# A cross-attention kernel: where GpSimd's sums of output weights, its head sums and its query powers stand

## The chip, the cores and the metric

The kernel runs on one core of a Trainium2 chip. The metric is device time in microseconds of one execution, median of several; the profile is of one further execution, which has a time of its own. The engines are TensorE (PE, with its weight loads PEld), VectorE (DVE), ScalarE (ACT), GpSimd (POOL) and SyncE (SP), which here issues almost every DMA in the order of its program.

## The reference, cut to what matters

```python
def _L0_xattn_ref(latents, context, Wq, Wk, Wv, Wo, q_norm_w, k_norm_w):   # 8 batches, 100 latents, 361 context rows
    kv = jnp.concatenate([context, latents], axis=1)                       # 461 keys
    q = (latents @ Wq)...            # 32 heads of 128
    k = (kv @ Wk)... ; v = (kv @ Wv)...                                    # 8 key heads, 4 query heads on each
    q = rms_norm(q, q_norm_w); k = rms_norm(k, k_norm_w)
    probs = jax.nn.softmax(einsum(qg, k) * scale)
    out = einsum(probs, v).reshape(bsz, q_len, HEADS * HEAD_DIM)
    return out @ Wo
x = x + jnp.tanh(g_xattn[0]) * _L0_xattn_ref(_layernorm(x), ctx_4096, ...)
x = x + jnp.tanh(g_ffn[0]) * _L0_ffn_ref(_layernorm(x), ...)               # router, top 2 of 8 experts of rank 16
```

## The kernel before, in words

Everything is float32. An operand is split into a high and a low part of TensorE's fp32r type (hi by ACT, lo = raw - hi by DVE), and a product is three matmuls (lines 973 to 975: hi*hi, hi*lo, lo*hi). The work has three stages.

**Keys and values** (until about 640 us). Seven Winograd products for each tile of rows. The keys and values go to DRAM (`kT_d`, `v_d`).

**Attention by units** (about 640 to 1470 us). A unit u is one key head and one batch (`UNITS` = 64 of them), and has four query heads. A query block n (`query_part(n, c)`, c = 0 to 7, n = 0 to 63) makes one query head for four batches, so two blocks share one head's weights, which SP loads (`load_wq`), and ACT and DVE split (`wq_split`). Nine blocks (`AHEAD`) are made before unit 0; then slot u of each engine's program holds the scores of unit u, the transposes and values of unit u-1, and query block u+9. In a slot:
- PE: `scores(u, i)` for the four heads into two banks, `turn_probs(u-1, t)` (transposes of the probabilities), `values(u-1, t)`, `query_part` and `squares` (a head's sums of squares).
- DVE (`slot`, for u below 55): `maxima(u, i)` (line 1923, and `nm` = -max * rq, line 1929), `inverse(u, i)` (`rr`, line 1938), `p_split(u-1, t)` (`pT_lo`, line 1917), `copy_queries`, and at the end of the slot `mean_squares` (`ms`, line 1887), `q_split(u+1)` (`q_lo`, line 1897) and, when u is odd and below 52, `next_wq` (`wq_lo`, line 1805). `scores(u+1, 0)` waits for `q_lo` of u+1.
- ACT: `exps(u, i)` waits for `nm`; `p_split`, `q_split`, `keep_attn(u-1)`.
- POOL: `scale(u, i)` (line 901) multiplies a head's probabilities by `rr` as soon as it is there. `turn_probs(u, 0)` in slot u+1 waits for all four. `unit_rms` (line 896) is the power -0.5 for four units at a time (`rq`), which `nm` needs. Before every fourth unit it stands ahead of that slot's scales. It waits for `ms`.

**The output product** by Winograd (from slot 56 on, alone after 1450 us). It wants sums of quarters of Wo and of attention outputs. These are made early, on POOL, between the scales:
- `weight_sum(i)`, i = 0 to 63 (line 912): step n = i // 4 of `WT_STEPS` = 16 takes one MB. SP loads it (`load_t(n)`, line 713) to one of two buffers `tb[:, n % 2]`, POOL makes four sums in place, and SP stores it (`store_t(n)`, line 717, to `wt_d`). `load_t(n)` for n >= 2 waits until the store of n-2 has landed; `store_t(n)` waits until the sums are made. `WT_AT` says after which slot's scales a sum stands: four ahead of slot 0 and behind `unit_rms(0)`, then one a slot and in every sixth slot or so two, until slot 50.
- `early_sum(n)`, n = 0 to 15 (line 918): a difference of two units' outputs (S3), loaded and stored by SP, one a slot behind the scales of slot 35 + n (`S3_AT` = 34 is the slot of the first load).

An engine works its program off in order, and a wait holds all behind it. Before unit 0, SP's program is: the last stores of keys, the loads of keys and values for units 0 and 1, `load_heads(n)` for n = 0 to 8 (which gives `load_wq(4)` at n = 5 and `load_wq(5)` at n = 7), with `load_t(0)` and `load_t(1)` at n = 7 (`AHEAD - 2`). `next_wq(7)` splits head 5's weights on ACT and DVE. On ACT it stands ahead of `q_split(0)`, and on DVE ahead of `mean_squares(6)`.

Of the kernel before, what the change touches and what calls it, by code (L numbers as in the profile page):

```python
# [15 lines left out]
B = 8  # L16
# [17 lines left out]
TB = B // 2  # L34
# [94 lines left out]
UNITS = G * B  # L129
AHEAD = 9  # L130
# [17 lines left out]
WT_OF = {P6: 0, P4: 1, P7: 2, P5: 3}  # L148
WT_OPS = ((2, 3, 2, True), (0, 2, 0, False), (3, 3, 0, True), (1, 1, 0, True))
WT_STEPS = GQ * R  # L150
WT_AT = {}
for _n in range(4 * WT_STEPS):
    WT_AT.setdefault(max(-1, (_n - 4) * 6 // 7), []).append(_n)
WT_DONE = {n: next(u for u in WT_AT if 4 * n + 3 in WT_AT[u]) for n in range(WT_STEPS)}

S3_AT = 34
S3_STEPS = GQ * TB

UPPER = (P5, P4)
TAIL0 = FIRST_OF[P2]  # L160
# [11 lines left out]
def build(nc, x, ctxT, Wq, Wkv, Wo, AR, BmT, vecs, rows, out):  # L172
    with ExitStack() as ctx:
        def sem(name):
            return ctx.enter_context(nc.semaphore(name))
# [203 lines left out]
        nm_done = sem("nm_done")  # L379
# [89 lines left out]
        def stored(u):  # L469

            return 16 * (u // 2 + 1)
# [29 lines left out]
        def _(sp):  # L501
# [112 lines left out]
            def load_kT(u):  # L614
                g, b = u // B, u % B
                if u >= 2:
                    sp.wait_ge(s_done, 4 * (u - 2) + 4)
                r0 = b // TB * ROWS_M + b % TB * NC
                l0 = b // TB * ROWS_M + CTX_M + b % TB * NQ
                src = kT_d[:, g]  # L620
                sp.dma_start(kT[:, u % 2, :, 0:NC].bitcast(F32), src[:, :, r0:r0 + NC]).then_inc(kT_in[u % 2], 16)
                sp.dma_start(kT[:, u % 2, :, NC:NK].bitcast(F32), src[:, :, l0:l0 + NQ]).then_inc(kT_in[u % 2], 16)

            def load_vv(u):
                g, b = u // B, u % B
                if u >= 2:
                    sp.wait_ge(pv_done, u - 1)
                r0 = b // TB * ROWS_M + b % TB * NC
                l0 = b // TB * ROWS_M + CTX_M + b % TB * NQ
                dst = vv[:, u % 2].bitcast(F32)  # L630
                sp.dma_start(dst[0:ROWS[0], 0], v_d[r0:r0 + ROWS[0], g]).then_inc(vv_in[u % 2], 16)
                sp.dma_start(dst[0:ROWS[1], 1:3], v_d[r0 + OFF[1]:r0 + NC, g].rearrange("(t r) l d -> r t l d", t=2)
                             ).then_inc(vv_in[u % 2], 16)
                sp.dma_start(dst[0:NQ, 3], v_d[l0:l0 + NQ, g]).then_inc(vv_in[u % 2], 16)

            def store_attn(u):
                sp.wait_ge(ao_done, u + 1)
                sp.dma_start(at_d[u // B, u % B], ao[:, u % 2]).then_inc(ao_stored[u % 2], 16)
# [13 lines left out]
            def load_heads_of(m):  # L652
# [6 lines left out]
                if m < 2:  # L659
                    for i in range(4):  # L660
                        sp.wait_ge(s3_stored[i], 16 * S3_STEPS // 4)
                elif o in (P5, P6) and c >= 2 or m - 2 > LAST_OF[P6]:
# [27 lines left out]
            def load_chunk(m):  # L690
                load_weights(m)
                load_heads_of(m)

            def load_s3(n):
                if n >= 4:
                    sp.wait_ge(s3_stored[n % 4], 16 * (n // 4))
                for th in range(2):
                    u = n // TB * B + th * TB + n % TB
                    sp.wait_ge(ao_stored[u % 2], stored(u))
                    sp.dma_start(s3b[n % 4][th], at_d[u // B, u % B]).then_inc(s3_in[n % 4], 16)  # L700

            def store_s3(n):
                sp.wait_ge(s3_sum, n + 1)
                sp.dma_start(s3_d[n // TB, :, n % TB], s3b[n % 4][0]).then_inc(s3_stored[n % 4], 16)
# [5 lines left out]
            def load_t(n):  # L710
                if n >= 2:
                    sp.wait_ge(t_stored[n % 2], 16 * (n // 2))
                sp.dma_start(tb[:, n % 2], Wo.rearrange("n (k c) p r d -> c r p (n k) d", k=2)[n // R, n % R]).then_inc(t_in[n % 2], 16)

            def store_t(n):
                sp.wait_ge(t_sum, 4 * n + 4)
                sp.dma_start(wt_d.rearrange("t c p r d -> c r p t d")[n // R, n % R], tb[:, n % 2]).then_inc(t_stored[n % 2], 16)
# [10 lines left out]
            def load_heads(n):  # L728

                h = n // 2 + 2  # L730
                if n % 2 == 1 and 4 <= h < H:
                    load_wq(h)

            for n in range(AHEAD):
                load_heads(n)
                if n == AHEAD - 2:
                    load_t(0)
                    load_t(1)
            for u in range(UNITS):
                load_heads(u + AHEAD)  # L740
                if 1 <= u < UNITS - 1:
                    load_kT(u + 1)

                for n in range(WT_STEPS):
                    if u == WT_DONE[n] + 1:
                        store_t(n)
                    if u == WT_DONE[n] + 2 and n + 2 < WT_STEPS:
                        load_t(n + 2)
                if 0 <= u - S3_AT - 2 < S3_STEPS:
                    store_s3(u - S3_AT - 2)  # L750
                if 0 <= u - S3_AT < S3_STEPS:
                    load_s3(u - S3_AT)
                if u in (OUT0 - 2, OUT0 - 1):
                    load_chunk(u - OUT0 + 2)
                if OUT0 + 1 <= u:
                    load_chunk(u - OUT0 + 1)
                if u == UNITS - 1:
                    load_heads_of(G + 2)
                    load_heads_of(G + 3)
                if u >= 1:  # L760
                    store_attn(u - 1)
                    if u + 1 < UNITS:
                        load_vv(u + 1)
# [50 lines left out]
        def _(pool):  # L814
# [76 lines left out]
            def unit_rms(u):  # L891

                g, b = u // B, u % B
                pool.wait_ge(ms_done, 2 * g + b // TB + 1)
                c = slice(R * b, R * (b + TB))
                pool.tensor_tensor(rq[0:NQ, g, c], ms[0:NQ, c], mhalf[0:NQ, 0:R * TB], ALU.pow).then_inc(rq_done, 1)

            def scale(u, i):
                a = 4 * u + i
                pool.wait_ge(rr_done, a + 1)  # L900
                pool.tensor_scalar(pr[0:NQ, u % 2, i], pr[0:NQ, u % 2, i], rr[0:NQ, i:i + 1], None,  # L901
                                   ALU.mult).then_inc(p_done, 1)

            def weight_sum(i):

                n = i // 4
                to, a, b, minus = WT_OPS[i % 4]
                if i % 4 == 0:
                    pool.wait_ge(t_in[n % 2], 16 * (n // 2 + 1))
                elif i % 4 < 3:  # L910
                    pool.wait_ge(t_sum, i)
                pool.tensor_tensor(tb[:, n % 2, to], tb[:, n % 2, a], tb[:, n % 2, b],
                                   ALU.subtract if minus else ALU.add).then_inc(t_sum, 1)

            def early_sum(n):

                pool.wait_ge(s3_in[n % 4], 32 * (n // 4 + 1))
                pool.tensor_tensor(s3b[n % 4][0], s3b[n % 4][0], s3b[n % 4][1], ALU.subtract).then_inc(s3_sum, 1)

            def chunk_sums(m):  # L920

                o, c = CHUNKS[m]
                pool.wait_ge(at_in[m % 4], a_loaded(m))
                if o == P6:
                    pool.wait_ge(at_sum, summed(m - 1))
                to, x, y = {P5: (a21[c % 2], a21[c % 2], a22[c % 2]), P6: (a11[c % 2], a21[c % 2], a11[c % 2]),
                            P3: (at_raw[m % 2], at_raw[m % 2], at_more[:, m % 2])}[o]
                for b in range(TB):
                    pool.tensor_tensor(to[:, b], x[:, b], y[:, b], ALU.add if o == P5 else ALU.subtract).then_inc(at_sum, 1)

            unit_rms(0)
            for i in WT_AT[-1]:
                weight_sum(i)
            for u in range(UNITS):
                if u % TB == TB - 1 and u + 1 < UNITS:
                    unit_rms(u + 1)
                for i in range(R):
                    scale(u, i)
                for i in WT_AT.get(u, ()):
                    weight_sum(i)  # L940
                if 0 <= u - S3_AT - 1 < S3_STEPS:
                    early_sum(u - S3_AT - 1)
                if u == UNITS - 2:
                    chunk_sums(FIRST_OF[P5])
            for m in range(FIRST_OF[P6], LAST_OF[P6] + 1):
# [1249 lines left out]
```

## Time and profile before

| | us |
|---|---|
| median of 3 runs | 1715.18 |
| lowest and highest | 1713.99, 1717.83 |
| the profiled execution's own time | 1715.65 |
| its span in the profile | 1713.8 |
| busy in the span: PE, DVE, POOL, ACT | 1665.8, 1239.6, 873.9, 865.1 |
| scores of unit 0 begin | 684.61 |
| scores of unit 51 begin | 1281.26 |

Times in the rows are microseconds from the start of the span. The profiled execution's time is 0.47 us above the median and 1.85 us above its own span. In the views by time a row gives start, duration, engine (a q behind it marks the queue that issues), line, operation, what is written and read, shapes and count, and in brackets the idle time before it with what ended it. Several instructions of a kind without a pause between them share a row. The view by stretches gives the stretch, its length, then busy time and count for PE, PEld, DVE, ACT and POOL, then PE's granted clock (1.00 is full), the DMA engines' busy share and GB/s. In it PE's busy time counts matmuls in their modelled length.

### The profile page before, as it was taken

What the parts mean: (1) busy time and instruction counts of PE and PEld (TensorE: products, weight loads), DVE (VectorE), ACT (ScalarE), POOL (GpSimd) and SP (SyncE); (2) the same over time, 40 slices, a digit from 0 to 9 for tenths busy, and PEclk for the clock granted to TensorE, in tenths of its full rate; (3) what the DMA queues carried; (4) which work ended last, traced back from release to release, by engine and by line L of the source; (5) the groups of instructions that cost most, each with busy time, mean ns of one, the idle gap of its engine ahead of it and who ended that gap; (6) DMA issues with size and microseconds to landing.
All of it is one profiled execution on the core that took longest, in us unless ns stands there. A gap on an engine that the chain in (4) does not pass through costs nothing.

```text
span 1713.8 us, 26112 instructions
## 1 busy us (share of the span) xinstructions
PE 1665.8 (97%) x9120; PEld 1475.3 (86%) x9120; DVE 1239.6 (72%) x2078; ACT 865.1 (50%) x1647; POOL 873.9 (51%) x668
## 2 busy tenths in 40 slices
PE   7999999999999999999999999999999999999996
PEld 6788888678888869899999999999999889999994
DVE  7788776677777742777777777777776876557767
ACT  5445554454444432555666565665555666443321
POOL 1454444134443320766767667788786445543320
PEclk9999999999999999999999999999999999999998
DMA  5667778636666564456555554666756557676632
GB/s 196 161 181 233 235 210 241 183 108 186 162 184 154 140 239 150 138 159 191 188 156 187 182 179 160 213 217 216 232 181 215 170 205 267 212 275 229 241 116 68
DMA packets 238502, 323.86 MB, mean 189 GB/s; under 512 B 53300, under 2 KB 193396, under 8 KB 233380
## 3 DMA queue, kind: packets, MB, share of 16 engines
q1 hardware_dynamic: 237796, 315.65, 59.8%
q10 hardware_dynamic: 576, 6.55, 0.9%
q8 instruction: 73, 1.20, 0.3%
q14 instruction: 57, 0.47, 0.1%
HBM read 212.18 MB, written 109.97 MB: 188 GB/s over the span
## 4 chain that ended last, share of the span: by engine, by line
PE 70%; DVE 18%; issue 4%; ACT 4%; DMA 2%; POOL 0%; DVEq 0%; SPq 0%; ACTq 0%; POOLq 0%
PE bank L973 21%; PE bank L975 20%; PE bank L974 20%; DVE mx L1923 4%; PE bank L1111 3%; DVE wq_lo L1805 3%; DVE q_lo L1897 3%; PE bank L1078 2%; DVE pT_lo L1917 2%; DMA kT_d<-kst 1%; PE bank L1007 1%; ACT pr L1539 1%; DVE q_raw L1875 1%; DVE nm L1929 1%; DVE wo_lo L1943 1%
## 5 line engine op out<-in xcount | busy, mean ns | idle before, releaser
L901 POOL TENSOR_SCALAR pr<-pr,rr 100x461 f32<-100x461 f32 x256 | 370.2, 1454 | 231.6 <-DVE rr L1938 231.6
L973 PE MATMUL bank<-w_hi,a_hi 128*128 128x512 f32 (+1 forms) x856 | 340.8, 398 | 11.7 <-DVE a_lo L1713 8.6
L975 PE MATMUL bank<-w_hi,a_lo 128*128 128x512 f32 (+1 forms) x856 | 334.8, 391 | 0.0
L974 PE MATMUL bank<-w_lo,a_hi 128*128 128x512 f32 (+1 forms) x856 | 334.3, 390 | 0.0
L1539 ACT ACTIVATE pr<-bank,nm,rq 100x461 f32<-100x461 f32 x256 | 188.8, 737 | 187.6 <-DVE nm L1929 186.2
L855 POOL TENSOR_TENSOR msk<-ssk,epst 128x4 f32<-128x4 f32 (+1 forms) x60 | 23.5, 391 | 348.5 <-DVE ssk L1744 348.5
L973 PEld LDWEIGHTS bank<-w_hi,a_hi 128*128 128x128 f32 (+1 forms) x856 | 157.8, 184 | 48.8 <-issue 9.7
L1923 DVE TENSOR_REDUCE mx<-bank 100x1 f32<-100x461 f32 x256 | 160.6, 627 | 48.7 <-PE bank L975 47.2
L975 PEld LDWEIGHTS bank<-w_hi,a_lo 128*128 128x128 f32 (+1 forms) x856 | 157.5, 184 | 38.0
L973 PE MATMUL bank<-xT_hi,wq_hi 128*128 128x400 f32 x512 | 188.9, 369 | 0.5 <-issue 0.5
L974 PEld LDWEIGHTS bank<-w_lo,a_hi 128*128 128x128 f32 (+1 forms) x856 | 158.0, 185 | 34.8
L975 PE MATMUL bank<-xT_hi,wq_lo 128*128 128x400 f32 x512 | 178.3, 348 | 0.0
L974 PE MATMUL bank<-xT_lo,wq_hi 128*128 128x400 f32 x512 | 178.2, 348 | 0.0
L973 PE MATMUL bank<-at_hi,wo_hi 128*128 128x400 f32 x448 | 159.9, 357 | 2.9 <-DVE at_lo L1954 2.5
L974 PE MATMUL bank<-at_lo,wo_hi 128*128 128x400 f32 x448 | 155.7, 347 | 0.0
L975 PE MATMUL bank<-at_hi,wo_lo 128*128 128x400 f32 x448 | 155.6, 347 | 0.0
L1530 ACT ACTIVATE pT_hi<-bank 120x400 fp32r<-120x400 f32 (+2 forms) x256 | 127.6, 498 | 52.2 <-PE bank L1111 51.4
L1917 DVE TENSOR_TENSOR pT_lo<-bank,pT_hi 120x400 fp32r<-120x400 f32 (+2 forms) x256 | 144.5, 565 | 8.0 <-ACT pT_hi L1530 7.6
L1111 PEld LDWEIGHTS bank<-ident,pr 100*120 100x120 f32 (+2 forms) x1024 | 111.1, 149 | 19.5 <-DVE pT_lo L1917 7.2
L1111 PE MATMUL bank<-ident,pr 100*120 100x100 f32 (+2 forms) x1024 | 122.3, 255 | 2.3 <-DVE pT_lo L1917 0.4
L1713 DVE TENSOR_TENSOR a_lo<-st,a_hi 128x512 fp32r<-128x512 f32 (+1 forms) x104 | 91.5, 881 | 34.8 <-ACT a_hi L1332 34.8
L1332 ACT ACTIVATE a_hi<-st 128x512 fp32r<-128x512 f32 (+1 forms) x104 | 63.2, 609 | 83.8 <-PE bank L975 73.6
(154 smaller groups left out, 3635.1 us busy)
## 6 DMA issues: line engine op xcount, KB each, us to landing
kT_d<-kst SPq DMA_DIRECT2D x56, 512.0 KB, 5.7
v_d<-vst SPq DMA_DIRECT2D x56, 512.0 KB
kT<-kT_d SPq DMA_DIRECT2D x64, 361.0 KB, 4.5
kvr<-ctxT SPq DMA_DIRECT2D x44, 512.0 KB, 6.2
wq_raw<-Wq SPq DMA_DIRECT2D x32, 512.0 KB, 5.8
tb<-Wo SPq DMA_DIRECT2D x16, 1024.0 KB, 8.3
wt_d<-tb SPq DMA_DIRECT2D x16, 1024.0 KB, 8.0
wo_raw<-wt_d SPq DMA_DIRECT2D x16, 1024.0 KB, 7.4
```

The lines of the kernel that those rows point to most:

```text
L901: pool.tensor_scalar(pr[0:NQ, u % 2, i], pr[0:NQ, u % 2, i], rr[0:NQ, i:i + 1], None, ALU.mult).then_inc(p_done, 1)
L973: pe.matmul(o, lh, rh, start=start, stop=False, skip_group_check=more)
L974: pe.matmul(o, lh, rl, start=False, stop=False, skip_group_check=more)
L975: return pe.matmul(o, ll, rh, start=False, stop=stop, skip_group_check=more)
L1111: mm = pe.transpose(ps[ptbank(u, t)][0:ROWS[t], i * NQ:(i + 1) * NQ], pr[0:NQ, u % 2, i, OFF[t]:OFF[t] + ROWS[t]], ident[0:NQ, 0:NQ])
L1332: act.activation(a_hi[:, i % RING, :, 0:cols(k % NT)], a_src(i), ACT.Copy).then_inc(a_hi_done, 1)
L1530: act.activation(pT_hi[0:ROWS[t], t], ps[ptbank(u, t)][0:ROWS[t], 0:QW], ACT.Copy).then_inc(pT_hi_done, 1)
L1539: act.activation(pr[0:NQ, u % 2, i], ps[BS[i % 2]][0:NQ, 0:NK], ACT.Exp, bias=nm[0:NQ, i:i + 1], scale=rq[0:NQ, g, R * b + i:R * b + i + 1 ...
L1713: dve.tensor_tensor(a_lo[:, i % RING, :, 0:n], a_src(i), a_hi[:, i % RING, :, 0:n], ALU.subtract).then_inc(a_lo_done, 1)
L1805: dve.tensor_tensor(wq_lo[:, h % 2], wq_raw[:, h % 2], wq_hi[:, h % 2], ALU.subtract).then_inc(wq_lo_done, 1)
L1917: dve.tensor_tensor(pT_lo[0:ROWS[t], t], ps[ptbank(u, t)][0:ROWS[t], 0:QW], pT_hi[0:ROWS[t], t], ALU.subtract).then_inc(pT_lo_done, 1)
L1923: dve.tensor_reduce(mx[0:NQ, i:i + 1], ps[BS[i % 2]][0:NQ, 0:NK], AX.X, ALU.max).then_inc(mx_done, 1)
```

## The change

- **Weights' sums.** Sixteen (steps 0 to 3) now stand on POOL ahead of `unit_rms(0)`, where there were four behind it. The other 48 stand one in each slot 0 to 47, not behind the scales but ahead of them, behind a wait for `nm` of the slot's first head.
- **Their transfers.** `load_t(0)` and `load_t(1)` move from n = 7 to n = 0 of SP's program before unit 0. At n = 5, 6, 7, 8 a `store_t` and a `load_t` follow: stores 0 to 3 and loads 2 to 5. So `load_wq(4)` stands ahead of `store_t(0)`, and `load_wq(5)` behind `load_t(3)`. In the slots `load_t(n+2)` comes right behind `store_t(n)`, not a slot later.
- **S3's sums.** Eleven stand behind the scales of slots 8, 12, ... 48, four behind `nm` in slots 48 to 51, and the last behind the scales of slot 52. SP loads a slot earlier and stores a slot later.
- **Powers.** `unit_rms` for units 4, 8, ... stands behind the scales two slots ahead of the unit (slots 2, 6, ...), where it stood ahead of the scales one slot ahead (3, 7, ...).

```diff
--- before.py
+++ after.py
@@ -148,13 +148,20 @@
 WT_OF = {P6: 0, P4: 1, P7: 2, P5: 3}
 WT_OPS = ((2, 3, 2, True), (0, 2, 0, False), (3, 3, 0, True), (1, 1, 0, True))
 WT_STEPS = GQ * R
-WT_AT = {}
-for _n in range(4 * WT_STEPS):
-    WT_AT.setdefault(max(-1, (_n - 4) * 6 // 7), []).append(_n)
-WT_DONE = {n: next(u for u in WT_AT if 4 * n + 3 in WT_AT[u]) for n in range(WT_STEPS)}
-
-S3_AT = 34
+
+WT_FIRST = 4
+WT_DONE = [4 * (n - WT_FIRST) + 3 for n in range(WT_STEPS)]
+WT_LAST = WT_DONE[-1]
+
+
 S3_STEPS = GQ * TB
+S3_TIMES = sorted([(u, 1) for u in range(B, WT_LAST + 6, TB)] + [(WT_LAST + 1 + n, 0) for n in range(4)])[:S3_STEPS]
+S3_AT = {t: n for n, t in enumerate(S3_TIMES)}
+S3_LOAD = {}
+S3_STORE = {}
+for _n, (_u, _i) in enumerate(S3_TIMES):
+    S3_LOAD.setdefault(_u - 1, []).append(_n)
+    S3_STORE.setdefault(_u + 1, []).append(_n)
 
 UPPER = (P5, P4)
 TAIL0 = FIRST_OF[P2]
@@ -733,23 +740,26 @@
 
             for n in range(AHEAD):
                 load_heads(n)
-                if n == AHEAD - 2:
+                if n == 0:
                     load_t(0)
                     load_t(1)
+                if n in (5, 6, 7, 8):
+                    store_t(n - 5)
+                    load_t(n - 3)
             for u in range(UNITS):
                 load_heads(u + AHEAD)
                 if 1 <= u < UNITS - 1:
                     load_kT(u + 1)
 
-                for n in range(WT_STEPS):
+                for n in range(WT_FIRST, WT_STEPS):
                     if u == WT_DONE[n] + 1:
                         store_t(n)
-                    if u == WT_DONE[n] + 2 and n + 2 < WT_STEPS:
-                        load_t(n + 2)
-                if 0 <= u - S3_AT - 2 < S3_STEPS:
-                    store_s3(u - S3_AT - 2)
-                if 0 <= u - S3_AT < S3_STEPS:
-                    load_s3(u - S3_AT)
+                        if n + 2 < WT_STEPS:
+                            load_t(n + 2)
+                for n in S3_STORE.get(u, ()):
+                    store_s3(n)
+                for n in S3_LOAD.get(u, ()):
+                    load_s3(n)
                 if u in (OUT0 - 2, OUT0 - 1):
                     load_chunk(u - OUT0 + 2)
                 if OUT0 + 1 <= u:
@@ -928,18 +938,23 @@
                 for b in range(TB):
                     pool.tensor_tensor(to[:, b], x[:, b], y[:, b], ALU.add if o == P5 else ALU.subtract).then_inc(at_sum, 1)
 
+            for i in range(4 * WT_FIRST):
+                weight_sum(i)
             unit_rms(0)
-            for i in WT_AT[-1]:
-                weight_sum(i)
             for u in range(UNITS):
-                if u % TB == TB - 1 and u + 1 < UNITS:
-                    unit_rms(u + 1)
+
+                if u <= WT_LAST:
+                    pool.wait_ge(nm_done, 4 * u + 1)
+                    weight_sum(4 * WT_FIRST + u)
+                if (u, 0) in S3_AT:
+                    pool.wait_ge(nm_done, 4 * u + 1)
+                    early_sum(S3_AT[u, 0])
                 for i in range(R):
                     scale(u, i)
-                for i in WT_AT.get(u, ()):
-                    weight_sum(i)
-                if 0 <= u - S3_AT - 1 < S3_STEPS:
-                    early_sum(u - S3_AT - 1)
+                if (u, 1) in S3_AT:
+                    early_sum(S3_AT[u, 1])
+                if u % TB == TB - 2 and u + 2 < UNITS:
+                    unit_rms(u + 2)
                 if u == UNITS - 2:
                     chunk_sums(FIRST_OF[P5])
             for m in range(FIRST_OF[P6], LAST_OF[P6] + 1):
```

## Rows read from the trace of the kernel before

**Rows 1.** The page's busy times: engine, busy us, share, instructions.

```profile
PE 1665.8 (97%) x9120; PEld 1475.3 (86%) x9120; DVE 1239.6 (72%) x2078; ACT 865.1 (50%) x1647; POOL 873.9 (51%) x668
```

**Rows 2.** Stretches from one unit's first scores to the next: units 26, 27 and 52.

```profile
988.62:1000.42 11.80, 11.71 (x74) 10.71 (x72) 9.65 (x19) 6.43 (x15) 7.08 (x6) 1.00 0.46 143
1000.42:1011.79 11.37, 11.37 (x73) 10.78 (x72) 8.58 (x19) 7.50 (x16) 10.22 (x7) 1.00 0.60 193
1292.65:1304.00 11.35, 11.35 (x73) 10.77 (x72) 7.79 (x19) 6.54 (x15) 5.75 (x4) 1.00 0.34 103
```

**Rows 3.** PE by time: the first matmul of the scores of units 2 and 51.

```profile
709.78 0.37 PE L973 MATMUL bank<-kT,q_hi 128*100 128x462 f32 x1
...
1281.26 0.38 PE L973 MATMUL bank<-kT,q_hi 128*100 128x462 f32 x1
```

**Rows 4.** DVE by time: the ends of slots 25 and 51.

```profile
986.59 1.59 DVE L1897 TENSOR_TENSOR q_lo<-q_raw,q_hi 128x400 fp32r<-128x400 f32 x1 [0.26 <-ACT q_hi L1519]
988.10 2.31 DVE L1805 TENSOR_TENSOR wq_lo<-wq_raw,wq_hi 128x1024 fp32r<-128x1024 f32 x1
...
1290.81 0.90 DVE L1897 TENSOR_TENSOR q_lo<-q_raw,q_hi 128x400 fp32r<-128x400 f32 x1 [0.26 <-ACT q_hi L1519]
1291.75 1.23 DVE L1805 TENSOR_TENSOR wq_lo<-wq_raw,wq_hi 128x1024 fp32r<-128x1024 f32 x1
```

**Rows 5.** POOL by time: sums and powers at the ends of slots 25, 26 and 51.

```profile
987.83 1.49 POOL L912 TENSOR_TENSOR tb<-tb 128x512 f32<-128x512 f32 x1
...
1001.23 2.93 POOL L896 TENSOR_TENSOR rq<-ms,mhalf 100x16 f32<-100x16 f32 x1
...
1290.64 1.45 POOL L901 TENSOR_SCALAR pr<-pr,rr 100x461 f32<-100x461 f32 x1 [0.37 <-DVE rr L1938]
```

**Rows 6.** DVE by time: unit 27's first `nm` and `rr`, and its third `nm`.

```profile
1002.04 0.16 DVE L1929 SCALAR_TENSOR_TENSOR nm<-mx,rq 100x1 f32<-100x1 f32 x1
...
1004.07 0.16 DVE L1938 RECIPROCAL rr<-rs 100x1 f32<-100x1 f32 x1
...
1005.83 0.59 DVE L1929 SCALAR_TENSOR_TENSOR nm<-mx,rq 100x1 f32<-100x1 f32 x1
```

**Rows 7.** Groups of POOL's instructions, forms kept apart: S3's sums (busy us, mean ns).

```profile
L918 POOL TENSOR_TENSOR at_raw<-at_raw 128x400 f32<-128x400 f32 x16 | 24.6, 1538 | 0.0
```

**Rows 8.** Waits of SP's queue, 640 to 1390 us: us in total, times, longest.

```profile
SPq L638 <- ACT ao L1546: 460.5, 58, 13.1
```

**Rows 9.** SP by time, before unit 0.

```profile
662.82 0.84 SPq L561 DMA_DIRECT2D wq_raw<-Wq  x2
663.70 1.91 SPq L713 DMA_DIRECT2D tb<-Wo  x2
```

**Rows 10.** DMA issues from 662.7 to 664.6 us: KB each, median us to landing.

```profile
tb<-Wo SPq DMA_DIRECT2D x2, 1024.0 KB, 11.0
```

**Rows 11.** The same of 690.0 to 690.5 us, then of 695.8 to 696.2 us.

```profile
wt_d<-tb SPq DMA_DIRECT2D x1, 1024.0 KB, 5.7
...
tb<-Wo SPq DMA_DIRECT2D x1, 1024.0 KB, 5.8
```

**Rows 12.** The same of 700 to 1300 us.

```profile
wt_d<-tb SPq DMA_DIRECT2D x15, 1024.0 KB, 8.1
```

**Rows 13.** POOL by time, before the scales of unit 0.

```profile
682.09 2.90 POOL L896 TENSOR_TENSOR rq<-ms,mhalf 100x16 f32<-100x16 f32 x1 [44.24 <-DVE ms L1887]
684.96 5.24 POOL L912 TENSOR_TENSOR tb<-tb 128x512 f32<-128x512 f32 x4
```

**Rows 14.** DVE by time, before unit 0 and in its first step.

```profile
680.70 1.23 DVE L1805 TENSOR_TENSOR wq_lo<-wq_raw,wq_hi 128x1024 fp32r<-128x1024 f32 x1 [0.38 <-ACT wq_hi L1438]
681.85 0.17 DVE L1887 TENSOR_SCALAR ms<-bank 100x16 f32<-100x16 f32 x1
...
686.20 0.16 DVE L1929 SCALAR_TENSOR_TENSOR nm<-mx,rq 100x1 f32<-100x1 f32 x1
```

**Rows 15.** The stretch in which PE's granted clock is low after unit 0.

```profile
694.75:701.57 6.82, 5.93 (x21) 5.38 (x22) 3.72 (x7) 1.73 (x4) 3.68 (x3) 0.50 0.77 219
```

## The prediction

> **What bounds the kernel now.** I read the page first, then the stretches from one unit's scores to the next, then DVE, POOL and SP by time at a slot's end and ahead of unit 0. TensorE is busy for 1665.8 of 1713.8 us [rows 1], so only what makes it wait, or run slowly, counts. In the attention stage PE repeats one slot of work. Unit 27's slot takes 11.37 us with PE busy throughout, unit 26's takes 11.80 us [rows 2]. It goes on like that: odd slots 11.37, even slots about 11.82. From unit 2 to unit 51 it is 1281.26 - 709.78 = 571.48 us for 49 slots [rows 3], a mean of 11.66. Slot 52, the first without a weights' sum ahead of it or in it, takes 11.35 [rows 2], though even. So PE's own work is 11.37 a slot, and every second slot loses about 0.45 us, a few of them more. Slot 51, odd and with `wq_lo` at its end, takes 1292.65 - 1281.26 = 11.39 [rows 2, 3].
>
> The loss comes from DVE at the end of odd slots. There DVE makes `q_lo` and then `wq_lo`, both with two inputs in SBUF. At the end of slot 25 they take 1.59 and 2.31 us, at the end of slot 51 0.90 and 1.23 [rows 4]. In slot 25 POOL goes from the last scale straight into a weights' sum at 987.83; in slot 51 the last scale, at 1290.64, has nothing behind it [rows 5]. The first maximum of the next unit stands behind `wq_lo` on DVE. In slot 25 `wq_lo` ends at 990.41, 1.79 us after the next scores have begun at 988.62 [rows 2, 4]; in slot 51 it ends at 1292.98, 0.33 after 1292.65, before the three matmuls of those scores are through. What the sum takes from DVE is (1.59 - 0.90) + (2.31 - 1.23) = 1.77 us, all of that lateness.
>
> **The slots after the change.** The sum leaves the slot's end, for the gap between `nm` and `rr` of the first head. In unit 27 that is from 1002.04 + 0.16 to 1004.07, 1.87 us [rows 6], and a sum takes 1.31 to 1.49 (the four in a row, 5.24 / 4, and the one at a slot's end) [rows 13, 5]. It ends before the scale could start, and DVE meanwhile mostly reads PSUM. So on POOL and on DVE I cost it at 0. If that cover were gone, it would be at most 1.49 us ahead of a unit's scales, a slot's length before PE wants the last of them. Odd slots keep only the last scale beside `q_lo`, which is slot 51's picture. Even slots get an S3 sum (1.54 us [rows 7]) or a power (2.93 us [rows 5]) behind the scales. They have no `wq_lo`, and the odd slots behind them take 11.37 even now, with a sum at the even slot's end, so 0 again. A power that began where slot 25's sum did, at 987.83, would end at 990.76 [rows 5]. By unit 27's timing `nm` comes 1.78 and `rr` 3.65 us after the scores' begin [rows 2, 6], so after 988.62 the next sum is due at 990.40 and starts 0.4 late, and is through at 992.25, when `rr` is due. The power's delay of the scales in slots 3, 7, ... goes; what it cost is inside the 571.48.
>
> SP: in slots 4, 8, ... 40 `load_t(n+2)` waits right behind `store_t(n)` for its landing, 8.1 us [rows 12]. Queued behind it are `store_attn`, `load_vv` and the next slot's keys. But SP waits for `ao` in every slot anyway, 460.5 / 58 = 7.9 us a time [rows 8]. I cost this at 0, or at up to 1 us of lateness for loads that have more than a slot of time.
>
> Gain of the slots: 571.48 - 49 x 11.37 = 571.48 - 557.13 = **14.4 us**, between 8 (half of it kept by new collisions) and 15.
>
> **The start, where the change costs.** `rq` of unit 0, and so `nm` and every exponential, now stands behind sixteen sums on POOL, and these behind a chain of transfers over two buffers. Before, `ms` came at 681.85, POOL's power started at 682.09, the four sums stood behind it, and `nm` came at 686.20 [rows 13, 14]. After:
> - `load_t(0)` goes out where the weights' loads did, at 662.8 [rows 9]. It is only 0.9 us earlier than now, since SP reaches it behind the keys' stores and loads. The two loads took 11.0 us with two weight loads ahead [rows 10], a load alone 5.8 [rows 11]. I take 7.7, as the keys and values of units 0 and 1 still move: 670.5.
> - Four sums, 5.24 [rows 13]: 675.7. `store_t(0)` waits for them.
> - The store lands after 5.7, alone [rows 11]: 681.5. Only then can `load_t(2)` go. `store_t(1)`, queued behind it, goes with it.
> - `load_t(3)` waits for that store. Load and store together are nearest to the 8.1 of the stage [rows 12], and issuing takes 0.4: 690.0.
> - It lands, beside `load_wq(5)`, after 7.0 (between 5.8 alone and 8.1): 697.0.
> - Four sums, 5.24: 702.3. The power, 2.90 [rows 13]: **705.2**.
>
> That is 19.0 us after 686.20. With the shortest landings everywhere (5.8, 5.7, 5.7, 5.8) it is 700.1, 13.9 late; with 11.0, 6, 9.5 and 8.5 it is about 710.5, 24 late. A second chain runs beside it. `load_wq(5)` stands on SP behind `load_t(3)`, so at 690.5, and lands after some 7 (half a MB beside a whole one). Head 5's split, now at 680.70 on DVE [rows 14], comes near 698. `ms` of blocks 6 and 7 and `q_split(0)` stand behind it: 700 to 701. It is hidden by the 702.3, and is next in line if POOL is sooner.
>
> In the first slot POOL's sum 16 wants `load_t(4)`, issued when `store_t(2)` lands, near 701.5, and so there near 709.6. The scales of unit 0 start near 711, 5.7 us after `nm`; now they start 4 after, behind the four sums. That, and the end of the collisions of those sums with `nm`, about cancel. PE's clock: after a wait of some 3 us for `q_lo` of unit 1 it is granted 0.50, the 1.2 GHz level, for 6.8 us, at 21 matmuls [rows 15]. Now the engine will have stood for 15 us ahead of unit 0. Its short work in slot 0 runs at that level too, mostly under waits: +1 (0 to 3).
>
> **The sum.** Against the profiled execution's own 1715.65: -14.4 + 19.0 + 1.0 = +5.6, so 1721.3. The median shown is 0.5 lower, so the forecast for a median is **1721**. A measurement of this kernel can tell about 0.2% (3.4 us) from no change.
>
> **Rivals.**
> - *A, the transfers are quick.* The chain is four transfers long, and each can land as when alone. The rows alone speak for it (5.7, 5.8 [rows 11]), those with company against it. The start then costs 13.9, and the time is 1715.65 - 14.4 + 13.9 + 0 to 1, 1715 to 1716. It ends as no change if the four landings sum to under some 26 us (I took 28.5), below 1712 only if also slot 0 gets shorter. Chance 0.24.
> - The Trainium skill, "DMA: Bandwidth & Descriptors", section "Anatomy of one DMA — SWDGE (gpsimd) path", has a fit for transfers that POOL issues: about 2.0 us fixed plus the bytes over 436 GB/s. That would be an estimate of 4.4 us for each MB here, four times that is 17.6, and by it the time would be near 1710. The store and the load alone, 5.7 and 5.8 us [rows 11], do not bear it out.
> - *B, the start is free, faster.* The sixteen sums would have to end before `ms` at 681.85. The time would be 1715.65 - 14.4 and some 2 for shorter first slots: 1699. It decides at a chain under 19 us from 662.8; even the shortest landings with two times 5.24 give 33.5. Only if SP came to `load_t(0)` far sooner would it hold, and the keys' stores ahead of it forbid that. Chance 0.05.
> - *C, the start costs more.* Landings of 9 to 11 us with the keys and weights beside, then `load_t(4)` late for sum 16, which holds the scales of unit 0, then PE at half clock: 24 + 4 instead of 20, so 1715.65 - 14.4 + 28 = 1729. Chance 0.13.
> - *D, the slots do not get clean.* The sum behind `nm` hits `nm` of the second head (0.16 us for the first head of unit 27, 0.59 for the third, beside a scale [rows 6]), or S3's sums and powers still hold DVE. Half the gain is lost: 1728. Against it: slots 51 and 52 [rows 2, 3]. Chance 0.08.
>
> **How the numbers follow.** The forecast has 0.50. Its own range, 1717 to 1726, lies to a fifth within 3.4 us of the present median. Same: 0.10 of it and 0.18 of A, 0.28. Faster: B, and 0.05 of A, 0.10. Slower: 0.40, C, D and a rest of A, 0.62. Cases of both signs exist but slower holds most. For 8 in 10 the range leaves out B and the edges of A and C: 1713 to 1730.
>
> **What the profile after would show.** Right: POOL's row of four sums splits into groups ahead of the power of unit 0, whose start moves from 682 to about 702; SP's `store_t(0)`, `load_t(2)`, `load_t(3)` near 676, 682, 690; `wq_lo` of head 5 near 698; PE idle for about 15 us ahead of unit 0; slots of 11.37 for both parities from unit 2 to 51, `q_lo` at 0.90 and `wq_lo` at 1.23 in odd slots. Wrong: the power of unit 0 starting before 690, even slots still at 11.8, or new waits of PE for keys or for `pr` in slots 4, 8, and so on.

## The result

| | before | changed |
|---|---|---|
| median us | 1715.73 (4 runs, 1713.99 to 1717.83) | 1732.26 (4 runs, 1726.71 to 1734.25) |
| ratio, 95% interval | | 1.0091 (1.0064 to 1.0117) |
| the profiled execution: its time, its span | 1715.65, 1713.8 | 1726.71, 1724.7 |

The changed kernel is slower by 0.9%, as forecast, but the median lies outside the range given (1713 to 1730). In a later set of four more runs it took 1727.23 (ratio 1.0064, interval 1.0047 to 1.0081). The profiled execution was the fastest of its set, 11.1 us over that of before.

With the first scores of units 2 and 51 as marks, the two profiles compare so:

| us | before | changed | difference |
|---|---|---|---|
| to the scores of unit 0 | 684.61 | 709.92 | +25.3 |
| units 0 and 1 | 25.17 | 21.43 | -3.7 |
| units 2 to 50 | 571.48 | 561.51 | -10.0 |
| unit 51 to the end | 432.5 | 431.8 | -0.7 |
| sum | 1713.8 | 1724.7 | +10.9 |

Some 2 us of the first row are not the change's: the first load of keys for unit 0, which the change does not touch, was issued at 658.2 before and at 660.2 after. In later runs of kernels with the same stage of keys and values it was between 657.5 and 660.1. The last row, which the change hardly touches, varies too: from 431.1 us (e5) to 436.3 (e3) over all profiles.

### The profile page after: what moved, and what is told of

Its sections match the earlier page's. It is cut to its first block, busy times and chain, and to the rows that moved or that the text cites. A ratio compares the mean times of both kernels' runs of the same rounds, so it can differ in the third digit from the quotient of the medians.

```text
span 1724.7 us, 26152 instructions
## 1 busy us (share of the span) xinstructions
PE 1655.3 (96%) x9120; PEld 1474.5 (85%) x9120; DVE 1190.0 (69%) x2078; ACT 867.8 (50%) x1647; POOL 860.0 (50%) x668
## 4 chain that ended last, share of the span: by engine, by line
PE 77%; DMA 7%; DVE 7%; ACT 3%; issue 3%; SPq 1%; POOL 1%; DVEq 0%; ACTq 0%; POOLq 0%
PE bank L988 23%; PE bank L990 22%; PE bank L989 22%; PE bank L1126 5%; DMA kT_d<-kst 2%; PE bank L1093 2%; DMA kT<-kT_d 2%; DMA wt_d<-tb 2%; PE bank L1022 1%; PE bank L1305 1%; POOL tb L922 1%; DVE wo_lo L1958 1%; DMA wq_raw<-Wq 1%; ACT w_hi L1370 1%; DVE y L2093 1%
## 5 line engine op out<-in xcount | busy, mean ns | idle before, releaser
L922 POOL TENSOR_TENSOR tb<-tb 128x512 f32<-128x512 f32 x64 | 84.2, 1319 | 130.9 <-DVE nm L1944 84.8
L1126 PE MATMUL bank<-ident,pr 100*120 100x100 f32 (+2 forms) x1024 | 116.2, 253 | 0.3 <-DVE pT_lo L1932 0.3
```

What stands on the lines that cost most here:

```text
L1126: mm = pe.transpose(ps[ptbank(u, t)][0:ROWS[t], i * NQ:(i + 1) * NQ], pr[0:NQ, u % 2, i, OFF[t]:OFF[t] + ROWS[t]], ident[0:NQ, 0:NQ])
```

## The profile after

The start, on POOL by time (it answers to [rows 13]):

```profile
673.18 11.42 POOL L922 TENSOR_TENSOR tb<-tb 128x512 f32<-128x512 f32 x8 [33.70 <-DMA tb<-Wo]
689.78 5.16 POOL L922 TENSOR_TENSOR tb<-tb 128x512 f32<-128x512 f32 x4 [5.18 <-DMA tb<-Wo]
701.53 6.03 POOL L922 TENSOR_TENSOR tb<-tb 128x512 f32<-128x512 f32 x4 [6.59 <-DMA tb<-Wo]
707.53 3.23 POOL L906 TENSOR_TENSOR rq<-ms,mhalf 100x16 f32<-100x16 f32 x1
```

The first eight sums run in a row, as both buffers were loaded. Each later group waits for a transfer, and the power of unit 0, at 682.09 before, starts at 707.53. What moved the transfers, on SP by time (to [rows 9]):

```profile
664.60 1.06 SPq L720 DMA_DIRECT2D tb<-Wo  x2
665.70 1.24 SPq L568 DMA_DIRECT2D wq_raw<-Wq  x1
678.45 0.37 SPq L724 DMA_DIRECT2D wt_d<-tb  x1
682.98 0.37 SPq L720 DMA_DIRECT2D tb<-Wo  x1
684.62 0.37 SPq L724 DMA_DIRECT2D wt_d<-tb  x1
692.68 0.37 SPq L720 DMA_DIRECT2D tb<-Wo  x1
693.09 0.51 SPq L568 DMA_DIRECT2D wq_raw<-Wq  x1
```

This is the staircase of the forecast, but for one step: `store_t(1)` did not go with `load_t(2)`. The store ahead had landed by 682.98, and the second four sums ended only at 684.60. The landings are in the view of DMA issues, one stretch for each of the four from 678 to 693 us (to [rows 10, 11]; the last column is us to landing):

```profile
wt_d<-tb SPq DMA_DIRECT2D x1, 1024.0 KB, 4.5
tb<-Wo SPq DMA_DIRECT2D x1, 1024.0 KB, 6.7
wt_d<-tb SPq DMA_DIRECT2D x1, 1024.0 KB, 8.0
tb<-Wo SPq DMA_DIRECT2D x1, 1024.0 KB, 8.8
```

With nothing else under way the store lands after 4.5, with the load beside it after 8.0. Head 5's query weights, issued at 693.09, hold ACT and, through it, DVE and PE (waits by who waited for whom, 640 to 1390 us; us in total, times, longest):

```profile
POOL tb L922 <- DMA tb<-Wo: 45.5, 3, 33.7
DVE wq_lo L1820 <- ACT wq_hi L1453: 28.5, 4, 21.5
ACT wq_hi L1453 <- DMA wq_raw<-Wq: 26.8, 2, 21.0
PE bank L1093 <- DVE ms L1902: 21.5, 1, 21.5
```

The last line is PE's: `squares(7)` waits for `ms`, behind the late split, and the last three of query block 8's eight parts stand behind `squares(7)`. When PE resumes, its clock is at the half level. The first row is 16 us in which PE does nothing, the others the slots of units 26, 27 and 9 (to [rows 2]):

```profile
685.00:701.00 16.00, 0.00 (x0) 0.00 (x0) 0.00 (x0) 0.00 (x0) 5.00 (x4) 0.61 0.81 227
...
1005.38:1016.79 11.41, 11.41 (x73) 10.85 (x73) 7.64 (x19) 6.54 (x15) 7.77 (x6) 1.00 0.48 148
1016.79:1028.19 11.40, 11.40 (x73) 10.81 (x72) 8.13 (x19) 7.49 (x16) 9.19 (x6) 1.00 0.44 137
...
810.91:823.20 12.29, 11.56 (x73) 10.65 (x71) 8.70 (x19) 8.00 (x17) 7.34 (x6) 1.00 0.75 211
```

The slots are clean for both parities, but not everywhere: unit 9's takes 12.29. DVE at the end of slot 25 (to [rows 4]):

```profile
1003.36 0.90 DVE L1912 TENSOR_TENSOR q_lo<-q_raw,q_hi 128x400 fp32r<-128x400 f32 x1 [0.26 <-ACT q_hi L1534]
1004.31 1.23 DVE L1820 TENSOR_TENSOR wq_lo<-wq_raw,wq_hi 128x1024 fp32r<-128x1024 f32 x1
```

Both are at their shorter times, 0.90 and 1.23 us. The slot that is still long is explained by PE's row at its end:

```profile
823.20 0.46 PE L988 MATMUL bank<-kT,q_hi 128*100 128x462 f32 x1 [0.73 <-DMA kT<-kT_d]
```

The keys of unit 10 came late. SP by time shows why (802 to 815 us), and the waits of its queue show how often (to [rows 8]):

```profile
802.18 0.47 SPq L724 DMA_DIRECT2D wt_d<-tb  x1
811.27 0.37 SPq L720 DMA_DIRECT2D tb<-Wo  x1
811.69 0.52 SPq L645 DMA_DIRECT2D at_d<-ao  x1
...
814.91 0.44 SPq L628 DMA_DIRECT2D kT<-kT_d  x1
```

```profile
SPq L645 <- ACT ao L1561: 358.6, 47, 13.2
SPq L720 <- DMA wt_d<-tb: 108.1, 14, 10.0
```

`load_t(6)` went out only when the store ahead of it had landed, 9.1 us behind it, and it went ahead of the attention output, the values and unit 10's keys. The keys were issued at 814.91, and PE, already waiting, began with them 8.3 us later. From 730 to 1345 us PE's weight loads waited 4.4 us for keys in all, six times, longest 1.2; units 10, 18, 26, 34, 38 and 42 had theirs no earlier than 0.06 us ahead of the scores' begin.

## The experiments

Two theories came out of this. **S**: the start costs some 20 us, because sixteen sums need stores and second loads between them. **Q**: in the slots, SP standing still behind a store, with one MB to load next, makes keys late. A third, **R**, is the forecast's gain: no sum behind the last scale. In the sets below, the kernel before took 1715.9 to 1716.7 on the same chips.

### e1: the loads a slot later

```diff
                     if u == WT_DONE[n] + 1:
                         store_t(n)
-                        if n + 2 < WT_STEPS:
-                            load_t(n + 2)
+                    if u == WT_DONE[n] + 2 and n + 2 < WT_STEPS:
+                        load_t(n + 2)
```

> The changed kernel with load_t(n+2) moved back to the slot behind its store_t(n), as before the change; all else stays. Theory Q (SP stands still behind a store that has not landed, so the keys of units 10, 14, 18, ... land at the last moment): the six waits of PE for kT (4.4 us in the profile of the changed kernel) go, units 2 to 51 take 557 us, and the time is about 4 to 5 us under the changed kernel's, about 1722 to 1727; if the changed kernel's runs of 1731 to 1734 come from the same waits, this one also spreads less. Rival (it is the amount that moves in these slots, not the standing queue): the keys still land 0 to 1 us ahead of need, and the time stays at 1727 to 1732. Both: the start stays as in the changed kernel, nm of unit 0 near 712.

Measured: 1722.47 (1721.91 to 1723.92), ratio 1.0039 (1.0025 to 1.0053). The stretch from unit 2's scores to unit 51's (columns as above):

```profile
730.29:1287.39 557.10, 557.10 (x3529) 528.67 (x3528) 395.88 (x919) 343.40 (x759) 391.02 (x269) 1.00 0.59 183
```

PE never waits in 557.10 us, and its weight loads wait for no key. The keys of unit 10 now go out at 811.13, ahead of `load_t(6)` at 812.07:

```profile
811.13 0.38 SPq L628 DMA_DIRECT2D kT<-kT_d  x1
811.55 0.47 SPq L629 DMA_DIRECT2D kT<-kT_d  x1
812.07 0.46 SPq L720 DMA_DIRECT2D tb<-Wo  x1
```

So Q holds: 4.4 us by the stretches of the profiles, 4.8 and 9.8 by the two medians of the changed kernel. (Of the 4.4, 3.9 stand at the units whose keys came late; 0.5 is slot 49, where a weight load waited for `pT_lo`. In the second profile of the changed kernel, e8, all of 4.5 stands at such units.) The amount moved is the same, so it was the standing queue and the order behind it; e1 changes both at once and doesn't tell one from the other. The spread was 2.0 us over five runs, where the changed kernel had 7.5 and 6.0 over four. That is no sign of the keys by itself: e5, whose keys are never late, spreads over 5.9.

### e2: head 5's query weights first

```diff
-                if n % 2 == 1 and 4 <= h < H:
+                if n % 2 == 1 and 4 <= h < H and h != 5:
                     load_wq(h)
+                if h == 4 and n == 5:
+                    load_wq(5)
```

> The changed kernel with the load of head 5's query weights issued right behind that of head 4, ahead of store_t(0). Theory S (the sixteen sums and their four transfers hold unit 0): the power of unit 0 still starts near 707 and ends near 710.4; only the part that waited for the weights goes, nm of unit 0 comes near 710.5 in place of 712.1, and the time falls by 1 to 3 us. Rival (the late query weights are what holds TensorE, 21.5 us of its waiting stand at squares(7) behind them): nm of unit 0 comes near 690 to 700 and the time falls by 10 us or more.

Measured: 1725.34 (1722.60 to 1729.81), ratio 1.0061 (1.0037 to 1.0084), 2 to 7 us under the changed kernel's medians. POOL by time:

```profile
689.08 5.16 POOL L924 TENSOR_TENSOR tb<-tb 128x512 f32<-128x512 f32 x4 [3.64 <-DMA tb<-Wo]
698.15 5.16 POOL L924 TENSOR_TENSOR tb<-tb 128x512 f32<-128x512 f32 x4 [3.92 <-DMA tb<-Wo]
703.27 2.90 POOL L908 TENSOR_TENSOR rq<-ms,mhalf 100x16 f32<-100x16 f32 x1
```

Unit 0's scores begin at 686.99, as if nothing had changed, and then its slot takes 29.6 us: the wait only moved behind them. `nm` comes at 706.21. Removing the one chain bares the other, and the rival of 10 us or more falls. I had put `nm` at 710.5. It comes 4 us sooner. From `store_t(0)` to the power it is 25.0 us for the 29.1 of the changed kernel: `load_t(3)`, which no longer shares its time with the query weights, takes 6.3 for 8.8 us, `store_t(1)` 6.4 for 8.0, and the last four sums 5.2 for 6.0; `store_t(1)` goes out 1.1 later.

### e3: the start alone

Into the kernel before, only the new start:

```diff
+WT_FIRST = 4
-    WT_AT.setdefault(max(-1, (_n - 4) * 6 // 7), []).append(_n)
+    WT_AT.setdefault(-1 if _n < 4 * WT_FIRST else (_n - 4) * 6 // 7, []).append(_n)
...
-                if n == AHEAD - 2:
+                if n == 0:
                     load_t(0)
                     load_t(1)
+                if n in (5, 6, 7, 8):
+                    store_t(n - 5)
+                    load_t(n - 3)
...
-            unit_rms(0)
             for i in WT_AT[-1]:
                 weight_sum(i)
+            unit_rms(0)
```

> The kernel before with only the start of the change: sixteen sums ahead of the power of unit 0, and SP's loads and stores of steps 0 to 5 ahead of unit 0 as in the changed kernel. The sums from 16 on stay where they were, behind the scales of slot 10 and after; powers and S3 as before. Theory S: unit 2 begins some 21 us later than in the kernel before (730 to 732 against 709.8), slots 2 to 9 run at 11.37 (gain 1.8 us), slots 10 to 50 as before: before + 18 to 20, 1734 to 1736, slower than the changed kernel. Rival (the start is hidden in part and the slots' new places are what costs): before + 0 to 8.

Measured: 1733.78 (1730.58 to 1735.90), ratio 1.0096 (1.0079 to 1.0113): +17.9 by the medians. Unit 2 begins at 728.49, 18.7 us later than before. The stretch to unit 51 takes 569.31, 2.2 less than before, as slots 2 to 11 run at 11.37. The time is at the low edge of the forecast (1734 to 1736), and S holds with nothing of the slots' change.

### e4: the slots alone

The new slots, with the start of before. The twelve sums that are no longer made ahead stand behind the scales of slots 0, 4, ... 44, where no `wq_lo` follows.

```diff
+WT_LAST = 47
+WT_AT = {(-1, 1): [0, 1, 2, 3]}
+_n = 4
+for _u in range(WT_LAST + 1):
+    for _i in (0, 1)[:1 + (_u % TB == 0)]:
+        WT_AT[_u, _i] = [_n]
+        _n += 1
...
+                for i in WT_AT.get((u, 0), ()):
+                    pool.wait_ge(nm_done, 4 * u + 1)
+                    weight_sum(i)
                 for i in range(R):
                     scale(u, i)
+                for i in WT_AT.get((u, 1), ()):
+                    weight_sum(i)
```

> The changed kernel's slots with the start of the kernel before: four sums behind the power of unit 0, load_t(0) and load_t(1) at n = 7; one sum behind nm in slots 0 to 47, and twelve more behind the scales of slots 0, 4, ... 44; load_t a slot behind its store. Powers and S3 as in the changed kernel. Theory S with Q: units 2 to 51 take 557 to 558 us against 571.5, the start costs nothing, and the time is 1715.7 - 14 = 1701 to 1703. Rival (sums in the gap between nm and rr cost what they save): units 2 to 51 take 565 us or more, time over 1708.

Measured: 1704.27 (1703.01 to 1706.90), ratio 0.9932 (0.9915 to 0.9949). It is the first version faster than before. From unit 2's scores to unit 51's:

```profile
712.39:1269.49 557.10, 557.10 (x3529) 528.69 (x3528) 399.14 (x919) 343.09 (x759) 406.29 (x280) 1.00 0.62 194
```

14.4 us less than before, the forecast's gain in full. Units 0 and 1 take 26.3 us, 1.2 more than before: five sums now stand in a row ahead of the first scales, which start 5.2 us after `nm`, and PE's weight loads wait 4.2 us at slot 1, where they waited 3.1 before.

### e5: four sums ahead of the power

```diff
+            for i in WT_AT[-1, 1]:
+                weight_sum(i)
             unit_rms(0)
-            for i in WT_AT[-1, 1]:
-                weight_sum(i)
...
+                if n == 0:
+                    load_t(0)
                 if n == AHEAD - 2:
-                    load_t(0)
                     load_t(1)
```

> e4_slots_only with the first four sums ahead of the power of unit 0 instead of behind it, load_t(0) at n = 0 for that, ahead of the query weights' loads, and load_t(1) behind them. The other 60 sums stay. Theory S: what costs at the start is only what ends after ms of unit 0 (about 683). Four sums end near 677 and so cost nothing; the collisions of the four sums with the first slot go, and with them the wait of slot 1 (4.6 us in e4) and part of the half clock behind it: scores of unit 2 begin at 707 to 709 in place of 712.4, time 1699 to 1701. Rival (any sum ahead of the power delays unit 0): nm of unit 0 moves later by 3 us or more and the time is 1704 or above.

Measured: **1699.13** (1695.41 to 1701.32), ratio 0.9900 (0.9884 to 0.9917). POOL by time:

```profile
670.88 6.10 POOL L926 TENSOR_TENSOR tb<-tb 128x512 f32<-128x512 f32 x4 [33.76 <-DMA tb<-Wo]
681.57 2.90 POOL L910 TENSOR_TENSOR rq<-ms,mhalf 100x16 f32<-100x16 f32 x1 [4.59 <-DVE ms L1908]
```

The sums end at 676.98. The power waits 4.6 us more, and for `ms`, not for them. (The 4.6 us that the forecast gave to e4's slot 1 were 4.2; of them 1.9 are left.) Unit 2 begins at 705.33, a bit sooner than I expected, though its stage of keys also ended early (first key load at 657.5). PE's clock, at the half level for 6.8 us after unit 0 before [rows 15], does not fall there at all. The twelve second sums still stand behind the scales of slots 0, 4, ... 44, and `q_lo` there takes 1.58 us. Yet slots 5, 9, ... take 11.39, as in e1. So a slow `q_lo` alone costs nothing; the loss needs `wq_lo` behind it, slowed too.

### e7: eight sums ahead

As e5, with `list(range(8))` ahead; the others from slot 2 on, ten of them as second sums.

> As e5, with eight sums (both buffers, no store between them) ahead of the power of unit 0; the other 56 stand one behind nm in slots 2 to 47 and ten behind scales of slots 4, 8, ... 40. Theory S: the eighth sum ends near 682 to 683, at the edge of ms of unit 0, so the start costs 0 to 2 us against e5, while sixteen, which need stores and second loads between, cost over 20. Time 1699 to 1703. Rival (the cost grows evenly with the number of sums, 24 us for sixteen): eight would cost some 12 us, time about 1710.

Measured: 1699.50 (1698.50 to 1703.63), ratio 0.9903 (0.9887 to 0.9920). The same as e5 by these runs.

```profile
672.33 12.30 POOL L926 TENSOR_TENSOR tb<-tb 128x512 f32<-128x512 f32 x8 [33.56 <-DMA tb<-Wo]
684.59 2.90 POOL L910 TENSOR_TENSOR rq<-ms,mhalf 100x16 f32<-100x16 f32 x1
```

The eighth ends at 684.6, the edge. So the cost is not by the sum: four and eight end alike in these runs, sixteen cost over 20 us more. From the first load of keys to unit 2's scores, which leaves out where the stage before ended, it is 51.6 us before the change, 47.8 in e5, 47.3 in e7, and 71.1 in the changed kernel. What sixteen need over eight is stores and second loads between the sums; where between eight and sixteen the cost sets in was not tried.

### e6: the sums behind the scales again

```diff
-                for i in WT_AT.get((u, 0), ()):
-                    pool.wait_ge(nm_done, 4 * u + 1)
-                    weight_sum(i)
...
-                for i in WT_AT.get((u, 1), ()):
+                for i in WT_AT.get((u, 0), []) + WT_AT.get((u, 1), []):
                     weight_sum(i)
```

> e4_slots_only with every weights' sum moved from the gap behind nm back to behind the slot's scales, ahead of S3's sums and powers, which keep their new places. It tells the place of the sums from the places of S3 and the powers. Theory R (a sum right behind the last scale slows q_lo and wq_lo of DVE at the end of odd slots): even slots go back to about 11.8, q_lo to 1.58 and wq_lo to 2.31 us, units 2 to 51 take 568 us or more, time 1715 or above. Rival (the powers ahead of the scales of slots 3, 7, ... were the loss): units 2 to 51 stay under 560 us, time under 1707.

Measured: 1714.48 (10 runs, 1711.41 to 1715.82), ratio 0.9987 (0.9977 to 0.9996). DVE at the end of an odd slot, and the stretch from unit 2 to 51:

```profile
1009.14 1.58 DVE L1914 TENSOR_TENSOR q_lo<-q_raw,q_hi 128x400 fp32r<-128x400 f32 x1 [0.27 <-ACT q_hi L1536]
1010.65 2.31 DVE L1822 TENSOR_TENSOR wq_lo<-wq_raw,wq_hi 128x1024 fp32r<-128x1024 f32 x1
```

```profile
709.49:1278.00 568.51, 566.33 (x3529) 526.99 (x3528) 443.93 (x919) 340.49 (x759) 413.06 (x281) 1.00 0.60 190
```

R holds, though the time is 0.5 us under the forecast's 1715. 568.51 - 557.10 = 11.4 us of the 14.4 are the place of the sums alone. The other 571.48 - 568.51 = 3.0 go with the powers' and S3's new places and with which slots hold a second sum; no run parts these. The late DVE reaches PE through `pT_lo`, the low part of the transposed probabilities. So wait PE's weight loads in the kernel before (730 to 1345 us):

```profile
PEld bank L973 <- DVE pT_lo L1917: 9.6, 26, 1.4
PEld bank L1111 <- DVE pT_lo L1917: 6.9, 24, 0.6
```

In e6 the two are 11.4 and 6.5 us, in 50 waits; in e1 there is one wait of 1.3, after unit 51.

### e8: the changed kernel once more

> The changed kernel once more, for a second profile: its other runs took 1731 to 1734, its profile was of the fastest, 1726.7. Theory Q: a slower run has the same start within 2 us and more or longer waits of TensorE for kT in the slots of units 2 modulo 4, so that units 2 to 51 take more than 561.5 us by what the time is above 1726.7. Rival: the start varies (longer landings of the chain), and units 2 to 51 stay at 561 to 562.

Measured: 1727.23 (1723.27 to 1729.28). Its profiled execution was again the fastest, 1723.27, so it does not tell what a slower run does. Units 2 to 50 take 561.55, as in the first, with waits for keys in other slots (5, 29, 41 the longest); the power of unit 0 starts at 703.88, 46.4 us after the first key load against 47.3. What sets the two profiles 3.4 us apart is all at the start: 2.7 us before the first load of keys, and 0.9 from there to unit 2. That is the rival's picture, but both were the fastest of their sets, so neither theory of the spread is decided.

## Why the prediction was right and wrong

- **The slots' gain, 14.4.** The mechanism and its size hold: DVE's `q_lo` and `wq_lo` shortened as said, and where nothing else came in (e1, e4, e5) the 49 slots took 557.10 against 557.13. In the changed kernel it was 10.0. In slots without `wq_lo` a slow `q_lo` (1.34 or 1.58 us) cost nothing, as said.
- **The step that failed: SP in slots 4, 8, ... 40, "I cost this at 0".** It cost 4.4 us in the profile (3.9 of it at the units with late keys), and 4.8 or 9.8 by the medians. I reasoned from SP's mean wait of 7.9 us for `ao` in a slot, that the store's landing would hide in it. It nearly did. But the wait ran 9.1 us in slot 8, the load of one MB then went out ahead of the outputs, values and keys, and all shared the DMA engines, so the keys of unit 10, issued 2.7 us later than in e1 (counted from unit 2's scores), also took longer. They had less than a slot of room, not "more than a slot": before, unit 10's keys were issued 10.1 us ahead of its scores, and the keys of units 3 to 53 landed 2.2 to 6.0 us ahead of need. The prediction has no row of that.
- **The start, 19.0 + 1.0 at unit 2.** Measured 731.35 - 709.78 = 21.6, of which 2.0 came before the first load of keys, so 19.6 for the 20.0. That it came so near is luck, as two parts were off and largely cancel. First, `nm` of unit 0 was 25.9 us late, 6.9 more than forecast. Of these 5.6 are the power's own end, 710.8 for 705.2: the chain began 1.8 later, `store_t(1)` waited 1.6 for the second four sums, `load_t(3)` took 8.8 for 7.0, and the last four sums 6.0 for 5.2; the lone store gave 1.2 back. The other 1.3 are the second chain, which was not hidden: I left out that PE's `squares(7)` waits behind it, with three parts of a query block at half clock after it. Second, slots 0 and 1 were 3.7 us shorter, where I had assumed that it "about cancels": slot 1 took 11.4 for 14.1, as its wait fell from 3.1 to 1.3 us and PE, at half clock there before [rows 15], ran it at the full level. The bounds of the chain were also added up wrong: the shortest landings give 699.6, not 700.1, and the longest 711.6, not 710.5, which moves A and C by 0.5 and 1.1 us.
- **Rivals.** A's landings did not come: a store alone took 4.5, but the chain's other three were never alone (6.7 to 8.8). The 5.7 that I called alone was not. SP issued the next unit's keys, 461 KB, right behind that store:

```profile
690.22 0.37 SPq L717 DMA_DIRECT2D wt_d<-tb  x1
690.63 0.51 SPq L621 DMA_DIRECT2D kT<-kT_d  x1
691.18 1.05 SPq L622 DMA_DIRECT2D kT<-kT_d  x1
```

The last of these keys landed 5.7 us after 691.18, so they also ran beside the first us of the load at 695.90, the 5.8 of rows 11.

The Trainium skill's fit for transfers that POOL issues ("DMA: Bandwidth & Descriptors", section "Anatomy of one DMA — SWDGE (gpsimd) path") gives an estimate of 4.4 us for one MB. The stores that were alone agree, 4.4 to 4.5 us in the changed kernel, e1, e2, e3 and e8, though SP issued them; so my sentence that rows 11 "do not bear it out" was a misreading. The three with company do not agree, and as the chain had company throughout, the fit is no price for a chain. B needed sums that fit ahead of `ms`. e5 and e7 are that case with four and eight sums, and come to B's 1699. D did not happen: `nm` of the second head took 0.16 us in the slots around unit 26.
- **The median.** The failed step (4.4), the later end of the stage before (2.0), the start (-0.4) and the end (-0.7) explain the profiled 1726.7 in place of 1721.3. It lies within the range. What took the first set's median 5.5 us further, and out of the range, stays open; the second set's was 0.5 further. The profiles show two stretches that vary by themselves, the stage of keys (2.7 us) and unit 51 to the end (5.2 us over all profiles); how often keys are late in the other runs is not shown.

## What to carry to other kernels

Moving work to a stretch where its engine is idle is free only while its inputs are there: price the chain of transfers over the buffers, not the instructions. A wait put on the queue that issues all loads is paid by whatever stands behind it, so look up for each load behind it how long ahead of need it lands. And an elementwise engine's short gap, here between `nm` and the first `rr`, can be the best place for work that slows another engine elsewhere.

## What was not expected of the hardware

- The same DVE instruction with two SBUF inputs beside POOL (`q_lo`) takes 0.57 us where it begins late in a scale (slots 56 to 62, in both profiles), 0.90 where it begins with the last scale and nothing follows or a power does, 1.34 with one of S3's sums behind the scale, and 1.58 with a weights' sum behind it, though at 0.90 it would have ended before that sum began, by the profile's times.
- One MB stored with nothing else under way landed in 4.4 to 4.5 us (changed kernel, e1, e2, e3, e8). With 461 KB of keys issued right behind it took 5.6 to 5.7 (before, e4, e6), and with one more MB under way 6.4 (e2) to 8.0 (changed kernel), and with one and a half MB under way 10.4 (changed kernel, the store at 694.97).
